# Expert stage of a decoder kernel: six down products interleaved earlier, and the router's transposes one product group later

## The reference, cut to what matters

```python
x = hidden_states.reshape(-1, HIDDEN)                     # 1024 x 256
router_logits = jnp.einsum('TD,DE->TE', x, gate)          # 32 experts
routing_weights = jax.nn.softmax(router_logits, axis=-1)
top_k_weights, top_k_indices = jax.lax.top_k(routing_weights, TOP_K)   # 4 of 32
...                                                       # normalized, zero elsewhere
gate_up = jnp.einsum('TD,EDF->TEF', x, gate_up_proj)      # F = 2 * 96
g, u = jnp.split(gate_up, 2, axis=-1)
gated = u * jax.nn.silu(g)
next_states = jnp.einsum('TEF,EFD->TED', gated, down_proj)
next_states = (next_states * router_weights[..., None]).sum(axis=1)
...
x = _layernorm(x + _L0_ffn_ref(x, ...), axis=-1)
```

## Time and profile before

| what | value |
|---|---|
| time, median of 3 runs | 834.44 us (834.16 to 835.54) |
| profiled execution, its own time | 835.06 us |
| its span, first to last instruction | 833.3 us |
| PE busy | 788.7 us, 95% of the span |
| DVE, POOL, ACT busy | 532.7, 379.5, 359.1 us |
| the expert stage, first gate matmul to last down matmul | 302.43 to 513.7 us |

### The profile page before, as it was taken

How to read it: one execution, slowest core, us unless ns; L and a number is a source line. 1 busy time by engine, 2 the same in 40 slices (tenths; PEclk the granted TensorE clock), 3 DMA queues, 4 the chain that set the end, 5 groups by cost and what they waited for, 6 DMA issues and landing times.

```text
span 833.3 us, 12743 instructions
## 1 busy us (share of the span) xinstructions
PE 788.7 (95%) x4140; PEld 606.6 (73%) x4140; DVE 532.7 (64%) x1042; ACT 359.1 (43%) x842; POOL 379.5 (46%) x345
## 2 busy tenths in 40 slices
PE   7899999999979989999999997988998998999997
PEld 5788888888854467888888885855555444788886
DVE  4766676677669975333333348669996698764535
ACT  3555555555551062323232334238998102544432
POOL 3221212123108934655555544578985796522100
PEclk9999999999989999999999999989999998899999
DMA  9410101010201114434342421000000012000001
GB/s 316 73 52 25 50 25 50 25 50 25 64 20 39 25 51 121 133 89 132 89 133 89 120 73 61 1 1 2 1 2 1 26 51 70 1 17 17 1 1 50
DMA packets 27055, 45.25 MB, mean 54 GB/s; under 512 B 3424, under 2 KB 16608, under 8 KB 26752
## 3 DMA queue, kind: packets, MB, share of 16 engines
q1 hardware_dynamic: 27008, 44.65, 18.0%
HBM read 43.45 MB, written 1.18 MB: 54 GB/s over the span
## 4 chain that ended last, share of the span: by engine, by line
PE 83%; DVE 10%; ACT 4%; issue 2%; DMA 1%; POOL 0%; DVEq 0%; ACTq 0%
PE bank L1602 11%; PE bank L1604 11%; PE bank L1603 11%; PE bank L1640 4%; PE bank L1641 4%; PE bank L1642 4%; PE bank L1627 3%; PE bank L1669 3%; PE bank L1673 3%; PE bank L1671 3%; PE bank L2136 2%; DVE arena L1377 2%; DVE mx L1386 2%; PE bank L2057 1%; PE bank L2050 1%
## 5 line engine op out<-in xcount | busy, mean ns | idle before, releaser
L1602 PE MATMUL bank<-xTh,ringh 128*128 128x512 f32 x420 | 168.5, 401 | 0.8 <-DVE xTl L1226 0.8
L1603 PE MATMUL bank<-xTl,ringh 128*128 128x512 f32 x420 | 165.3, 394 | 0.0
L1604 PE MATMUL bank<-xTh,ringl 128*128 128x512 f32 x420 | 165.3, 393 | 0.0
L1295 DVE TENSOR_TENSOR arena<-bank,arena 128x512 f32<-128x512 f32 x48 | 33.2, 691 | 114.8 <-ACT arena L917 105.6
L1604 PEld LDWEIGHTS bank<-xTh,ringl 128*128 128x128 f32 x420 | 78.8, 188 | 18.7
L1602 PEld LDWEIGHTS bank<-xTh,ringh 128*128 128x128 f32 x420 | 79.1, 188 | 16.3 <-issue 1.4
L1603 PEld LDWEIGHTS bank<-xTl,ringh 128*128 128x128 f32 x420 | 78.9, 188 | 15.0
L646 POOL TENSOR_TENSOR arena<-arena 128x512 f32<-128x512 f32 x48 | 62.6, 1305 | 51.9 <-DVE HTl L1299 49.3
L917 ACT ACTIVATE arena<-bank 128x512 f32<-128x512 f32 x48 | 28.7, 598 | 125.8 <-PE bank L1604 125.7
L569 POOL CAST ringh<-ring 128x768 fp32r<-128x768 f32 x15 | 13.3, 885 | 149.5 <-DMA ring<-w_attn 149.2
L1640 PE MATMUL bank<-outh,HTh 128*128 128x256 f32 x192 | 54.9, 286 | 3.1 <-DVE outl L1116 1.2
(11 more groups left out here) (293 smaller groups left out, 1956.3 us busy)
## 6 DMA issues: line engine op xcount, KB each, us to landing
ring<-w_moe SPq DMA_DIRECT2D x24, 256.0 KB, 3.0
arena<-route SPq DMA_DIRECT2D x16, 384.0 KB, 4.0
ring<-w_attn SPq DMA_DIRECT2D x15, 384.0 KB, 3.0
toep<-toep SPq DMA_DIRECT2D x32, 128.0 KB, 2.0
arena<-route SPq DMA_DIRECT2D x16, 256.0 KB, 4.3
outring<-w_down SPq DMA_DIRECT2D x24, 128.0 KB, 2.0
outring<-wo_attn SPq DMA_DIRECT2D x16, 128.0 KB, 2.0
arena<-route SPq DMA_DIRECT2D x16, 128.0 KB, 4.0
```

Source lines behind the costliest of these rows:

```text
L1602: pe.matmul(o, ringh[:, slot, wc], xTh[:, k, halves[j]], start=(k == 0), stop=False)
L1603: pe.matmul(o, ringh[:, slot, wc], xTl[:, k, halves[j]], start=False, stop=False)
L1604: ins = pe.matmul(o, ringl[:, slot, wc], xTh[:, k, halves[j]], start=False, stop=(k == DK - 1))
```

## The change

Three functions now give, for a position i, how many down products are done behind it:

- `downs_through(i)`: PE, behind `ups(i)`. Up to i = 26 it is i - 8, as before. At i = 27, 30, 33, 36, 39 and 42 it grows by two. Behind `ups(47)` there are now `downs(44)`, which belongs to that position, and three more.
- `highs_through(i)`: the halves on ACT and DVE, `downs_through(i + 1)`, so that at i = 26, 29, 32, 35, 38 and 41 two high halves and two low halves are done.
- `routed_through(i)`: POOL, two beyond `highs_through(i)`, from i = 8 on.

`turn_router()` moves behind `gates(5)`. The SP list is the same.

```diff
+def downs_through(i):
+    return max(0, i - LAG + max(0, min(CATCH_MOST, (i - CATCH_UP) // 3 + 1)))
+def highs_through(i):
+    return downs_through(i + 1) if i < NP0 - 1 else NP0
+def routed_through(i):
+    return min(NP0, highs_through(i) + 2) if i >= LAG else 0
...
+CATCH_UP, CATCH_MOST = 27, 6
...
             for n in range(2, NB0):
-                k = 2 * n - 2 - LAG
-                if k >= 0:
+                for k in range(routed_through(2 * n - 5), routed_through(2 * n - 4)):
                     routed(k)
                 split_moe(n, n % 2)
-                if k >= 0:
-                    routed(k + 1)
-            for k in range(2 * NB0 - 2 - LAG, NP0):
+                for k in range(routed_through(2 * n - 4), routed_through(2 * n - 3)):
+                    routed(k)
+            for k in range(routed_through(2 * NB0 - 5), NP0):
                 routed(k)
...
-                if i >= LAG:
-                    high_half(i - LAG)
-                if i % 2 == 1 and i >= 7:
-                    high_down((i - 7) // 2)
-            for k in range(NP0 - LAG, NP0):
-                high_half(k)
-                if k in (41, 43, 45):
-                    high_down((k + 1) // 2)
+                if i == LAG - 1:
+                    high_down(0)
+                for k in range(highs_through(i - 1), highs_through(i)):
+                    high_half(k)
+                    if k % 2 == 1 and k < NP0 - 2:
+                        high_down((k + 1) // 2)
...
+                for k in range(highs_through(i - 1), min(highs_through(i), NP0 - 1)):
+                    low_half(k)
+                    if k % 2 == 0 and k <= NP0 - 8:
+                        low_down(k // 2)
+                    if k in (NP0 - 7, NP0 - 5, NP0 - 3):
+                        low_down((k + 1) // 2)
...
-            turn_router()
             for i in range(5, NP0):
                 gates(i)
+                if i == 5:
+                    turn_router()
                 ups(i)
-                if i > LAG:
-                    downs(i - LAG - 1)
-            for k in range(NP0 - LAG - 1, NP0):
+                for k in range(downs_through(i - 1), downs_through(i)):
+                    downs(k)
+            for k in range(downs_through(NP0 - 1), NP0):
                 downs(k)
```

More of the change, by code:

```diff
@@ L1314, in _ @@
             dve.tensor_copy(rwT[:, 0:HALF], bank[0:NE0, 5, :]).then_inc(rwt_done, 1)
-            for i in range(5, LAG):
+            for i in range(5, NP0):
                 gated(i)
[L1317 to L1325, removed]
+                for k in range(highs_through(i - 1), min(highs_through(i), NP0 - 1)):
[4 more added lines that the diff above has]
+                        low_down((k + 1) // 2)
             norm(2, down_done, [NP0 - 2] * 2 + [NP0] * 2, apart=True)
```

## The result

| kernel | median, us | lowest to highest, runs | ratio, 95% interval |
|---|---|---|---|
| before | 834.16 | 833.46 to 836.98, 11 | |
| changed | 830.07 | 826.88 to 833.53, 11 | 0.9949, 0.9931 to 0.9967 |

The forecast was 829.6, with a range of 827.7 to 832.3. The profiled execution of the changed kernel took 829.97 us, its span 828.2.

A forecast was written before the change was run, and what follows sets the result against it. PE, busy 95% of the span, was taken as the bound. Stage end 3.65 plus router net 1.15 gave 4.8 us: 835.06 to 830.3 profiled, or 829.6 from the median 834.44; range 827.7 to 832.3 (own range 828.8 to 830.4).

The forecast's parts named there:

- its own signs of being wrong: PE waiting for HTl or outl at positions 27 to 42, or at downs(0) by over 0.5 us.
- rival B: Factors land late for the moved products: up to 2.6 us lost, 832.2 us; chance 0.17, its slower end 0.04.
- (1): End of the expert stage: six down products leave it, worked out one by one, gain 3.65 us.
- The second way: End of the stage: six steps that cost 2.00 us and then 1.43, 6 x 0.57 = 3.4 us gain.
- (2): Second halves on ACT and DVE at i = 26, 29, ...: hidden with 2.1 us of slack, cost zero.
- Rival D: PE waits for second low halves at the six new places, 0.57 us each: 833.0 us; chance 0.09.
- (5): Factors for routed(36) and routed(38), asked for earlier: cost zero at downs(38), with 1.4 us to spare.
- (3): Router: gates(5) fills 1.40 of the 1.47 us wait ahead of the transposes, so PE is 1.40 us ahead.
- (4): routed(0) behind split_moe(5): low_half(0) meets routed(1) and downs(0) starts 0.25 us late; bounds 0 and 1.4.
- Rival C: The router's lead is lost at downs(0), no gain from (3): 830.8 us; chance 0.10.
- The bound of 2.6: Most that late factors cost at downs(38), in us, if landings take 6.0 us, the longest: 2 x 2.0 - 1.4.
- Rival A: Low-clock stretch behind the stage, about 1.6 us, goes missing or comes twice: 828.0 or 831.2 us; chance 0.15.

The follow-up runs named there:

- e7_again: The changed kernel with no edit, measured and profiled once more: 828.08 us, ratio to before 0.9939.
- e4_three: The changed kernel with three doubled positions (27, 30, 33) in place of six: 826.60 us, ratio to before 0.9914.
- e3_sp: The changed kernel with factors and down weights issued on SP ahead of gate and up weights from block 20 on: 828.69 us, ratio to before 0.9937.
- e1_router: The kernel before with only the router's transposes moved behind gates(5): 832.01 us, ratio to before 0.9979.
- e2_tail: The changed kernel with the router's transposes back ahead of gates(5): 829.08 us, ratio to before 0.9958.
- e5_seven: The kernel of e3_sp with seven doubled positions from 24 on, in place of six from 27 on: 828.96 us, ratio to before 0.9947.
- e6: The kernel before with routed(k), for k of 41 and more, multiplying only 8 of 512 columns: 829.35 us in one run.

## Why the prediction was right

The prediction came within 0.5 us of the median, and T to A within 0.9 of its sum. That the time is the nearer of the two is luck: the same kernel's median was 828.08 in e7_again. One of its own signs of being wrong came up, a wait of PE at downs(38), which it had given to rival B; it was a small one. By its own steps:

- **(1), the end of the stage: 3.65 worked out, 3.56 measured** (15.88 - 8.58 - 3.74). Every step held, to 0.13 at most. The second way, 6 x 0.57 = 3.4, holds for the products as such: 0.58 each between e4_three and e3_sp.
- **(2), the cover at the six places: right.** PE shows no wait for a second half at 27, 30, 33, 36 or 39. Rival D, 833.0, fell with that; e4_three shows for its three that they cost 1.43 each. The place at 42 is the exception, and its cause is (5).
- **(3), the router: 1.40 of lead, right.** T to D and the restart give 1.14 where 1.15 was forecast. The wait left ahead of the transposes is 0.23, not some 0.1; the transposes wait for DVE's chain, so this moves nothing.
- **(4), downs(0) late by 0.25: the number and the mechanism right, the cause too narrow.** e1_router loses 0.34 without moving routed(0). Rival C, the whole lead lost, is ruled out.
- **(5), the factors: the term that was mis-sized.** Zero was taken, with 1.4 us to spare; it was 0.7 us in the trace, 0.5 in the second. Rival B is what happened, in small. By the prediction's clock low_down(19) was to end 1.4 us ahead of PE; it ended 0.2 behind: 22.7 us behind the end of ups(37) (480.74 - 458.07) for 21.0, 1.7 late. About 0.6 of that is the split, which met DVE (L608 took 1.70 us at 468.98) and ended at 12.6 for 12.0. About 0.7 is the two issues, 2.12 us for 1.09, and a landing 6.2 us behind the split's end where 5.1 to 5.5 had been allowed. The rest is POOL and DVE meeting behind it. The bound of 2.6 held. What the sum left out was load_down(19): ACT waits for it with silu(41) behind, and it was in SP's list behind the factors all the time.
- **Rival A, the clock: true in kind, and larger than priced, though not shown to come from the earlier start.** 1.6 us was taken for one stretch more or less. Behind A it was 2.4 us between the two profiled executions, at the stage's start 2.3 the other way, and runs of one kernel lay 7 us apart (before and changed), once 12 (e2_tail). The median of many runs is what the forecast met; the single profiled spans would have credited the change with 5.1.
- The start from 834.44 gave 0.3 us: before measured 834.16.

In sum: 3.56 + 1.14 - 0.7 = 4.0 against 3.95 measured; the 0.85 us missing from 4.8 are the late factors (0.7), and 0.1 at the end.

## What to carry to other kernels

Work that stands in a loop of two buffers at the end of a stage (2.0 us a piece) can be done at the bound engine's own rate (1.43) where that engine is busy; price it as the difference times the pieces, and then go through the last few one by one. Before pulling it forward, follow every DMA that it and its neighbours need from the instruction that lets SP issue it, with the longest issue and landing that the trace has, and write down who stands behind each wait. Leave room beyond that: in e5_seven factors landed after up to 8.5 us, where the trace of before had 6.0. The cover gave out at the sixth place and cost more than the piece brought at the seventh. Compare two traces by distances between anchors where the clock is the same in both, never by spans alone.

## What had not been expected of the hardware

- The two issues of a block's factors took 0.89 to 1.09 us in most places, but in the changed kernel 1.89, 1.70 and 2.12 in three, all behind load_moe on SP's queue; the trace of before has one of 1.56. Nothing in the traces says why.
- PE loses more than the gap when it waits: the first matmul of 256 columns behind a gap of 0.1 to 1.5 us is followed by the next after 0.18 to 0.23 us, not 0.12, so each wait costs up to 0.1 more. All ten traces show it.
- The clock behind the stage. Traces of e2, e4, e5 and e6 had 6.8 us at the lower level there, the changed kernel (twice), e3 and e1 13.7, the kernel before 23.9 and 17.1; over these the rest grows from 318.0 to 323.1 us. What decides it stays open: the same code gave two values in the kernel before and one in the changed. The Trainium skill (TensorE: Matmul & The Clock Gate, "What's actually happening") puts the cost of warming up at under 1% of a typical span, not to be fitted in a model. The trace agrees, 5 of 830 us at most; but the change is worth 0.5%, and a single trace can hide or double it.
